# A gated expert kernel in float32: shared weights come a second time for splitting, unit 0's raw weights get their own room, and the first samples come by three queues

## The reference, cut to what matters

```python
def _dense(x, wi_, wo_):
    return jax.nn.relu(x @ wi_) @ wo_          # 256 -> 1024 -> 256
s0 = _dense(x, swi[0], swo[0])
s1 = _dense(x, swi[1], swo[1])
h = relu(einsum('bsd,bdf->bsf', x, wi[type_label]))
eo = einsum('bsf,bfd->bsd', h, wo[type_label])
gate_in = concatenate([eo[:, 0], s0[:, 0], s1[:, 0]], axis=-1)
w = softmax(relu(gate_in @ g1) @ g2, axis=-1)[:, :, None, None]
x = x + eo * w[:, 0] + s0 * w[:, 1] + s1 * w[:, 2]
x = x + zX * lap_x(x) + zY * lap_y(x) + zR * x * (1 - x)
```

## Time and profile before

| | |
|---|---|
| median of three runs | 1152.47 us (1152.13 to 1152.71) |
| the profiled execution's own time | 1154.09 us |
| its span in the trace | 1152.6 us |
| PE busy | 1140.2 us (99%) |
| DVE busy | 675.4 us (59%) |
| ACT busy | 453.8 us (39%) |
| POOL busy | 72.8 us (6%) |
| read from HBM | 85.20 MB |

### The profile page before, as it was taken

One profiled execution on the slowest core, in us unless ns is written; L12 is line 12 of the kernel. 1 busy time (PEld: TensorE's weight loads), 2 busy tenths in 40 slices (PEclk: granted clock), 3 DMA queues, 4 the chain that ended last, 5 costly groups with the idle time before them and its releaser, 6 DMA issues.

```text
span 1152.6 us, 16891 instructions
## 1 busy us (share of the span) xinstructions
PE 1140.2 (99%) x6088; PEld 974.2 (85%) x6088; DVE 675.4 (59%) x1035; ACT 453.8 (39%) x798; POOL 72.8 (6%) x115
## 2 busy tenths in 40 slices
PE   7999999999999999999999999999999999999998
PEld 6888888888888888888888888888888888888888
DVE  5765656656665644555555565565465565556556
ACT  2555545545555532323323423333333333333333
POOL 1111111111111100000000000000000000000001
PEclk9999999999999999999999999999999999999999
DMA  6645466455555514022121131230230230221200
GB/s 205 203 139 172 128 181 189 147 155 175 164 176 156 165 33 124 12 73 45 49 74 31 59 78 25 59 83 20 64 84 12 71 74 20 73 50 43 75 28 24
DMA packets 110100, 107.64 MB, mean 93 GB/s; under 512 B 78313, under 2 KB 87106, under 8 KB 110018
## 3 DMA queue, kind: packets, MB, share of 16 engines
q1 hardware_dynamic: 96658, 59.64, 19.2%
q0 software_dynamic: 12800, 46.41, 13.3%
q10 hardware_dynamic: 560, 0.53, 0.2%
HBM read 85.20 MB, written 17.04 MB: 89 GB/s over the span
## 4 chain that ended last, share of the span: by engine, by line
PE 98%; DVE 1%; DMA 1%; issue 0%; ACT 0%; SPq 0%; POOL 0%; DVEq 0%; POOLq 0%
PE acc L849 31%; PE hbank L822 16%; PE hbank L821 16%; PE hbank L823 16%; PE acc L850 16%; PE tbank L777 1%; PE acc L746 1%; DMA rw<-in_L_cond_wi 1%; PE acc L861 0%; PE acc L863 0%; PE acc L862 0%; PE tbank L773 0%; PE tbank L778 0%; PE tbank L785 0%; PE acc L835 0%
## 5 line engine op out<-in xcount | busy, mean ns | idle before, releaser
L539 DVE SCALAR_TENSOR_TENSOR hl<-hbank,hh 128x512 fp32r<-128x512 f32 (+2 forms) x440 | 275.7, 627 | 434.7 <-ACT hh L949 434.2
L949 ACT ACTIVATE hh<-hbank 128x512 fp32r<-128x512 f32 (+2 forms) x440 | 240.7, 547 | 597.5 <-PE hbank L823 594.5
L849 PE MATMUL acc<-swo,hh 128*128 128x512 f32 x992 | 359.3, 396 | 0.0
L850 PE MATMUL acc<-swo,hl 128*128 128x256 f32 x992 | 277.8, 280 | 0.0
L849 PEld LDWEIGHTS acc<-swo,hh 128*128 128x128 f32 x992 | 186.3, 188 | 43.7
L821 PE MATMUL hbank<-xh,swh 128*128 128x512 f32 (+1 forms) x528 | 205.3, 389 | 0.0
L822 PE MATMUL hbank<-xl,swh 128*128 128x512 f32 (+1 forms) x528 | 205.0, 388 | 0.0
L823 PE MATMUL hbank<-xh,swl 128*128 128x512 f32 (+1 forms) x528 | 202.1, 383 | 0.0
L850 PEld LDWEIGHTS acc<-swo,hl 128*128 128x128 f32 x992 | 187.1, 189 | 9.6
L849 PE MATMUL acc<-ewo,hh 128*128 128x512 f32 x528 | 194.5, 398 | 0.3
L850 PE MATMUL acc<-ewo,hl 128*128 128x256 f32 x528 | 148.0, 280 | 0.0
(11 more groups left out here) (188 smaller groups left out, 895.9 us busy)
## 6 DMA issues: line engine op xcount, KB each, us to landing
rw<-in_L_cond_wi POOLq DMA_DIRECT2D x44, 512.0 KB, 4.3
rw<-in_L_cond_wo POOLq DMA_DIRECT2D x44, 512.0 KB, 4.5
xs<-in_x SPq DMA_DIRECT2D x128, 64.0 KB, 3.2
eo_scratch<-eo SPq DMA_DIRECT2D x128, 64.0 KB, 2.4
xs<-in_x SPq DMA_DIRECT2D x16, 512.0 KB, 4.4
rw<-in_x SPq DMA_DIRECT2D x256, 32.0 KB, 2.2
ei<-eo_scratch SPq DMA_DIRECT2D x16, 512.0 KB, 5.6
out<-ot SPq DMA_DIRECT2D x15, 512.0 KB, 6.4
```

Of the source, the lines that this page charges most:

```text
L539: e.scalar_tensor_tensor(HL[:, g % NH, 0:w], bank[:, 0:w], 0.0, HH[:, g % NH, 0:w].bitcast(F32), ALU.max, ALU.subtract).then_inc(h_lo, 1)
L849: e.matmul(acc[j][:, 0:2 * D], HH[:, g % NH, js], woc[:, c, :], start=(c == 0), stop=False)
L850: m = e.matmul(acc[j][:, D:2 * D], HL[:, g % NH, js], woc[:, c, 0:D], start=False, stop=last)
L949: e.activation(HH[:, g % NH, 0:w], hbank[g % HRING][:, 0:w], ACT.Relu).then_inc(h_hi, 1)
```

## The change

- The shared weights of passes 0 and 1 stay raw. They are loaded a second time, one piece in the pass of each of the units 4, 6, 8, 10, 11, 13, 15 and 17 (`SHARED_AT`), into a new buffer `RX`, and split at chunk 3 of that pass (high part) and chunk 4 (low part). POOL issues these loads (`load_shared`) behind the unit's own.
- Unit 0's raw weights get buffers of their own, `RW0`, where the second `EWO` lies later; unit 1's go to `RW`. So unit 0's loads wait for nothing but the table, and unit 1's splitting of pieces 2 and 3 waits until unit 0's piece 3 is split.
- Unit 0's samples: ACT issues three, SP three and POOL two, these between its pieces 0 and 2.
- The table: `tab`'s samples row is written first and read straight from PSUM; `ROWS_AT` goes from 4 to 6.
- `WARM` goes from 14 to 6 and the transposes of row 0 stand ahead of the counts.
- ACT takes over the copy of row 0 and the relus of the first eight chunks from DVE (`EARLY`).
- Unit 0's transposes move to (2, 0), into two free `acc` banks (`tile_bank`). The last two second products of pass 1 stand behind them and ahead of the first product of pass 2. "gate s" moves to (2, 5).
- `XF`, `HF` and `S01` become parts of `RX`.

```diff
-ROWS_AT = 4
-WARM = 14
+ROWS_AT = 6
+WARM = 6
+
+EARLY = 8
 LAST_ORDER = (0, 2, 1, 3)
+
+FIRST_BY = {"ACT": (0, 1, 2), "SP": (3, 4, 5), "POOL": (6, 7)}
...
-FIRST_CUTS = {(0, 4): [(0, 0)], (0, 5): [(0, 2)], (0, 6): [(0, 1)], (0, 7): [(0, 3)], (1, 3): [(2, 0)], (1, 6): [(2, 2)],
-              (2, 0): [(1, 0)], (2, 1): [(1, 1), (2, 1)], (2, 2): [(2, 3)], (2, 4): [(1, 3)], (2, 7): [(1, 2)]}
...
+SHARED_PIECES = [(ws, p) for ws in range(2) for p in range(4)]
+SHARED_AT = (4, 6, 8, 10, 11, 13, 15, 17)
+FIRST_HIGH = {(1, 6): [(2, 0)], (2, 0): [(2, 2)], (2, 1): [(2, 1)], (2, 3): [(2, 3)]}
+FIRST_LOW = {(1, 7): [(2, 0)], (2, 0): [(2, 2)], (2, 2): [(2, 1)], (2, 4): [(2, 3)]}
...
+    if c == 3 and n - 2 in SHARED_AT:
+        out.append(SHARED_PIECES[SHARED_AT.index(n - 2)])
...
-            e.wait_ge(x0_prod, 1)
-            e.tensor_copy(XF[:].rearrange("p k n -> p (k n)"), acc[1][:, 0:256]).then_inc(x0_done, 1)
...
+                if (n, c) == (2, 0):
+                    second_product(g - 2)
+                    second_product(g - 1)
                 if g < G:
                     first_product(g)
...
+            e.wait_ge(x0_prod, 1)
+            e.activation(RX[:, 0:256], acc[1][:, 0:256], ACT.Copy).then_inc(x0_done, 1)
...
+                if g < EARLY:
+                    e.wait_ge(h_prod, g + 1)
+                    if g >= NH:
+                        e.wait_ge(*h_free(g - NH))
+                    e.activation(HF[:, g % NH, :], hbank[g % HRING][:, 0:128], ACT.Relu).then_inc(h_early, 1)
...
-                    e.wait_ge(*cut_done(0 if ws == 2 else ws - 1, p))
-                    if ws == 2:
-
-                        if p:
-                            e.wait_ge(x_in[1], X_VAL[1])
+                    if ws == 3:
+
...
+            e.wait_ge(dve_seq, AT["experts"])
+            load_unit(0, (0,))
+            for b in FIRST_BY["POOL"]:
...
+            load_unit(0, (2, 1, 3))
             for u in range(1, NU):
                 load_unit(u, (0, 2, 1, 3))
+                if u in SHARED_AT:
+                    load_shared(SHARED_AT.index(u))
```

More of the change, by code:

```diff
@@ L226, in cond_resid_program @@
             EWL = [sb(f"ewl{i}", [128, 2, F], F32R, early) for i in range(2)]
-            EWO = [sb(f"ewo{i}", [128, NC, 2 * D], F32R, early) for i in range(2)]
+            EWO = [sb("ewo0", [128, NC, 2 * D], F32R, early)]
+            with ExitStack() as first:
+                RW0 = [sb(f"rw0{i}", [128, 1024], F32, first) for i in range(4)]
+            EWO.append(sb("ewo1", [128, NC, 2 * D], F32R, early))
             RW = [sb(f"rw{i}", [128, 1024], F32, early) for i in range(4)]
@@ L684, in _ @@
                     gate_spread()
+                if (n, c) == (2, 0):
+                    cut_low(2, 2)
                 if g < G:
```

157 lines of the change are left out of this document (93 added, 64 removed).

## The result

The changed kernel takes **1146.37 us** (median of five runs, 1145.9 to 1148.54) against 1152.47 us before (five runs, 1152.13 to 1153.71). The ratio is 0.9948, with a 95% interval of 0.9934 to 0.9963. It is faster by 6.1 us, where 10.15 were forecast, and it lies 0.07 us above the upper end of the range. The profiled execution took 1146.6 us, so that trace against trace the gain is 1154.09 - 1146.6 = 7.5 us.

What follows compares the result with a forecast made beforehand. PE, busy 1140.2 of 1152.6 us, bounds the kernel, so only the first 37 us can gain. Chunk (2, 2) starting 10.8 us earlier, less 0.63, gives 10.15 off the 1152.47 us median: 1142.3 us, range 1140.6 to 1146.3.

Steps and rivals of the forecast that it cites:

- landmark: First product of chunk (2, 2), at 36.58 us before; forecast at 25.8, 10.8 us earlier, with no PE wait behind it.
- The table: Start, slot calculation: fewer warm-up products and less DVE work make the samples' row ready at 11.6 us, 4.5 us earlier.
- rival A: Start: PE's full clock comes later after six warm-up products, or a hole lowers it; 1144.0 to 1146.0 us, chance 0.2.
- The `pre` passes: Passes ahead of unit 0: ten chunks behind the rows cost 8.8 us, products up to (1, 7) end at 20.0 us.
- The first samples: Unit 0's samples, issued on three queues: last landing at 19.5 us, taking 4 us to land.
- Rival B: Start: samples, weights and shared weights share full engines, loads land 3 to 4 us late; 1145.3 to 1146.3 us, chance 0.14.
- The sum: Start: chunk (2, 2) comes 10.8 us earlier, less 0.63 us for "gate s" put behind it, leaving 10.15 us.
- the start's saving is the same for both: Last step: the 10.15 us, worked out on the profiled execution (1154.09 us), is taken from the median, 1152.47 us.
- The second coming: Eight unit passes: reloading and splitting shared pieces, 4.2 MB, hides in idle time and costs nothing; uncovered, 2.3 us a piece.
- Late next: Unit 1's samples, needed before chunk (2, 3), and its first piece are on the edge; taken as 0, at most 1 us.
- C: Rival: a load, above all unit 1's samples, gains only 4.5 us and PE loses 8 to 10; 1150.2 to 1154.8, chance 0.03.
- D: Rival: the eight splits delay hidden values so that PE waits in those passes; up to 1160.4 us, chance 0.03.

Runs made afterwards that it cites:

- a_early0: Changed kernel with all relus of the first two passes on DVE (`EARLY = 0`); 1146.8 us.
- b_rw0: Kernel before with only a room of its own for unit 0's raw weights; 1157.17 us, ratio 1.0033.
- a_xfirst: Changed kernel with POOL's two samples issued ahead of unit 0's piece 0; 1148.19 us.
- a_fonly: Changed kernel plus two filler products, with unit 1's weights and samples and unit 0's pieces 2, 1, 3 held until unit 0's samples on ACT's and SP's queues landed; 1152.76 us.
- a_evac: Changed kernel with DVE's copy of the second gates' row moved from chunk (2, 1) to (2, 0); 1146.71 us.
- b_again: Kernel before, unedited, run again for a second trace; 1152.86 us.
- a_double: Changed kernel with each split of the eight reloaded shared pieces made twice, on ACT and on DVE; 1147.68 us.

## Why the prediction was right and where it was wrong

**What bounds it** held: all of the gain lies ahead of the landmark, and PE waits nowhere behind 30 us.

**The table.** Counts read at 5.62 us (forecast 5.55), slot's one-hot from 10.49 (10.1), rows at 10.92 (10.7), the samples' row ready at 12.08 (11.6). The pace of the first chunks was as forecast in that trace and as in rival A in others.

**The first weights.** Issued at 13.63 (13.1), in ACT's hands at 18.56 (19.0), 4.9 us where I had taken 5.9. Right.

**The `pre` passes** ended at 20.93 (20.0): 0.2 us is a slip of the sum (11.4 and 8.8 are 20.2), 0.3 us came up to the end of the rows, where PE waited for the one-hot, and the rest in the chunks behind. Mis-sized by 0.9. By itself this costs nothing, since the samples landed later still; a_early0 shows it with 1.2 us more.

**The first samples.** This step failed: "I put the last landing at 19.5 (4 us as for samples in that stretch)". The 4 us match the longest landing of ACT's samples in the trace before:

```profile
DMA to landing us min/median/max: 2.2/2.9/4.1
```

In that trace the four samples that ACT and SP issued ahead of POOL's first piece (18.72) took 2.2 to 2.7 us, the four behind it 3.5 to 5.0, in a stretch with half-empty engines. With the change seven of the eight go out behind the piece (13.63), and more loads behind them; those seven took 3.7 to 6.1 us, and the last landing was 22.1, 2.6 later than forecast. PE waited 1.08 us. The step counted issue times, which it had nearly right (16.03 for ACT's last, 15.4 forecast), and took the landing from a row whose condition the change itself removes. Rival B had named the mechanism, loads in line, with 3 to 4 us. b_rw0 shows what POOL's pieces alone do to the samples, a_xfirst what their order does, and a_fonly that 5.2 of the 6.1 us stay without any load behind. Why a sample behind one 512 KB piece takes so long stays open. By the Trainium skill (DMA: Bandwidth & Descriptors, "Issuing engines are not separate DMA queues") the three issuers share the same 16 engines; the runs agree (65, 16 and 8% of them for the three queues in a_fonly from 16 to 18 us).

**The sum.** PE began the transposes at 22.18 us where the sum has 20.0. Of these 2.2 us the forecast had 0.3 in hand (22.0 and 0.7 are 22.7, and 23.0 was taken), and the landmark is 1.93 us later than 25.8. Behind it "gate s" costs its 0.63. (By the starts in the timeline "gate s" costs 0.39 and the landmark moved by 8.61; the two differences cancel.) Then comes a wait for which the sum has no term: "freed only ACT and DVE, which PE did not wait for there: nothing". The first second product of unit 0 waits for DVE's copy of the second gates' row, which stands behind two hidden values on DVE; before, PE had waited 1.41 us for that same copy. It costs 0.6 us (a_evac). So 10.15 - 1.93 - 0.6 = 7.6, against 7.5 trace against trace.

**From trace to median.** The second step that failed: "the start's saving is the same for both". The profiled execution was 1154.09 - 1152.47 = 1.62 us slower than the median. Against b_again 1.3 us of this are seen, all in the start: 0.6 from the longer warm-up and about 0.7 from the half clock at 14 to 17 us; the other 0.3 are not accounted for. The change removed this loss, and I counted it as saved from a median that never had it. The changed kernel's trace is 0.23 us above its own median: 7.5 - 1.62 + 0.23 = 6.1 us. With this step alone put right the forecast is 1143.9 us; with the landing of the samples and the copy right too, 1143.94 + 1.93 + 0.6 = 1146.5.

**The second coming** costs nothing, as forecast, and not even doubled (a_double). **Late next**: no wait at (2, 3), as taken. **Rival A** is true of some executions, at 1.5 us, where 1.7 to 3.6 were given; **B** of all, smaller (1.9 us of landmark); **C** and **D** of none. That the result lies at the upper end of B's 1145.3 to 1146.3 is chance: the 1.6 us of the median and the 0.6 of the copy are no part of B.

## What to carry to other kernels

A landing time holds for the load on the engines at which it was read. Where a change fills a stretch in which they were idle, count the bytes that must have landed by each need, and not the issues, and look which small loads now stand behind a large one. Look at which kind of execution the profiled one is before you subtract a saving from a median: where its own time is 1.6 us above the median, find the stretch in which it lost them, and see whether the change touches it. A second trace of the same kernel shows it at once.

## What was not expected of the hardware

- The same kernel has PE at full pace from 5.8 us in one execution and from 10.9 us in another, with the same instructions. With one product of 128 columns ahead of the counts and one behind them no trace of six is late, where five of nine without them are.
- In the kernel before, waits of 1.16 and 0.82 us between 11 and 14 us were followed by 1.2 GHz (granted clock 0.51) in one trace and not in another (b_again, 1.00). The warm-up had taken 0.6 us longer in the trace that fell.
- A 64 KB sample issued ahead of a 512 KB piece of POOL's queue took 2.2 to 2.7 us (a_xfirst), one issued up to 2.4 us behind it 3.7 to 6.1 (after), and 7.8 behind four of them (b_rw0). In a_fonly one took 5.2 us although the engines moved 3 packets in its last 1.5 us. What sets the share of the engines among the queues was not tried.
